# VectorE takes a block of exps ahead of the low parts of K, V, Q and the output products

## What is computed

```
x = layernorm(x + causal self attention(x))      32 heads of 16, rope
q = x Wq + bq                                    32 query heads of 128, 256 rows
k, v = split(context Wkv + bkv)                  8 K and V heads, 4 query heads to each
a = softmax(q k' / sqrt(128))                    over 1601 keys
x = layernorm(x + (a v) Wo + bo)
x = layernorm(x + x Wb' + top-2-of-28 experts' low-rank products)
```

## Time and profile before

| | us |
|---|---|
| median of three runs | 2960.67 |
| lowest, highest | 2955.37, 2963.62 |
| the profiled execution | 2956.6 |
| its span, first to last instruction | 2954.8 |

### The profile page before, as it was taken

How to read it: one execution, slowest core, us unless ns; L and a number is a source line. 1 busy time by engine, 2 the same in 40 slices (tenths; PEclk the granted TensorE clock), 3 DMA queues, 4 the chain that set the end, 5 groups by cost and what they waited for, 6 DMA issues and landing times.

```text
span 2954.8 us, 60508 instructions
## 1 busy us (share of the span) xinstructions
PE 2760.3 (93%) x20272; PEld 2576.1 (87%) x20272; DVE 2100.3 (71%) x4364; ACT 1973.2 (67%) x4392; POOL 1660.6 (56%) x1663
## 2 busy tenths in 40 slices
PE   7899999998899999999899999999988999999996
PEld 6789999998679999999768999999967899999995
DVE  5477777778557878787755877777766587878785
ACT  4476676767457777677655877777756576767673
POOL 4288897947115656565611656555552265656564
PEclk9999999999899999999999999999989999999998
DMA  5446464612311212121331112121232121212112
GB/s 186 139 165 216 160 231 158 211 58 101 119 48 44 94 51 94 51 94 51 122 102 44 63 67 76 69 74 71 78 119 86 42 74 57 89 55 90 55 55 100
DMA packets 97921, 285.10 MB, mean 96 GB/s; under 512 B 9936, under 2 KB 18256, under 8 KB 94416
## 3 DMA queue, kind: packets, MB, share of 16 engines
q1 hardware_dynamic: 97616, 281.24, 27.3%
HBM read 237.16 MB, written 44.04 MB: 95 GB/s over the span
## 4 chain that ended last, share of the span: by engine, by line
PE 67%; issue 11%; POOL 9%; ACT 5%; DVE 5%; DMA 2%; DVEq 0%; ACTq 0%; SPq 0%; POOLq 0%
PE bank L1030 39%; PE dn L1030 14%; PE sp L1030 9%; POOL kept_s L527 4%; ACT ph L714 2%; PE sp L1161 1%; POOL orw L546 1%; PE sp L1169 1%; POOL ol L550 1%; ACT pn L641 1%; PE sp L1101 1%; PE sp L1248 1%; DVE mcol L909 1%; POOL hib L517 1%; ACT sp L719 1%
## 5 line engine op out<-in xcount | busy, mean ns | idle before, releaser
L527 POOL TENSOR_TENSOR kept_s<-kept_s,mrow 128x512 f32<-128x512 f32 (+1 forms) x896 | 1062.3, 1215 | 596.8 <-ACT mrow L704 596.7
L920 DVE TENSOR_TENSOR pl<-sp,ph 128x512 fp32r<-128x512 f32 (+1 forms) x896 | 576.9, 644 | 79.3 <-ACT sp L719 75.8
L714 ACT ACTIVATE ph<-kept_s 128x512 fp32r<-128x512 f32 (+1 forms) x896 | 534.1, 596 | 45.7 <-POOL kept_s L527 42.8
L719 ACT ACTIVATE sp<-kept_s 128x512 f32<-128x512 f32 (+1 forms) x896 | 506.1, 565 | 2.1 <-DVE sua L928 2.1
L1030 PE MATMUL dn<-ph,vh 128*128 128x256 f32 (+1 forms) x1664 | 489.4, 294 | 2.2 <-DVE pl L920 1.7
L1030 PE MATMUL dn<-ph,vl 128*128 128x256 f32 (+1 forms) x1664 | 471.4, 283 | 0.0
L1030 PE MATMUL dn<-pl,vh 128*128 128x256 f32 (+1 forms) x1664 | 470.7, 283 | 0.0
L928 DVE TENSOR_TENSOR sua<-sp,sua 128x512 f32<-128x512 f32 (+1 forms) x640 | 400.2, 625 | 0.0
L696 ACT ACTIVATE kept_s<-bank 128x512 f32<-128x512 f32 x384 | 228.5, 595 | 232.0 <-PE bank L1030 231.4
L696 ACT ACTIVATE kept_s<-sp 128x512 f32<-128x512 f32 x384 | 228.6, 595 | 193.0 <-PE sp L1030 192.6
L1030 PEld LDWEIGHTS dn<-ph,vh 128*128 128x128 f32 (+1 forms) x1664 | 316.5, 190 | 10.3 <-DVE pl L920 3.4
(11 more groups left out here) (149 smaller groups left out, 6967.4 us busy)
## 6 DMA issues: line engine op xcount, KB each, us to landing
wqx<-wq SPq DMA_DIRECT2D x128, 512.0 KB, 3.3
wox<-wo SPq DMA_DIRECT2D x64, 1024.0 KB, 4.8
wk<-wk SPq DMA_DIRECT2D x32, 512.0 KB, 3.3
wvx<-wv SPq DMA_DIRECT2D x16, 1024.0 KB, 5.6
raw<-in_ctx_t SPq DMA_DIRECT2D x48, 200.0 KB, 2.4
wqk<-in_ws SPq DMA_DIRECT2D x17, 513.0 KB, 4.0
raw<-in_wq_in SPq DMA_DIRECT2D x32, 256.0 KB, 3.8
wq<-hib SPq DMA_DIRECT2D x32, 256.0 KB, 2.0
```

Source lines behind the costliest of these rows:

```text
L527: nc.gpsimd.tensor_tensor(kept_s[:, n % 2, i:z, :], kept_s[:, n % 2, i:z, :], mrow[:, n % 2, :].unsqueeze(1).broadcast_to([P, z - i, S]), ...
L714: nc.scalar.activation(ph[:, k % PH, 0:cols], src, ACT.Exp, scale=XSCALE).then_inc(ph_ok, 1)
L719: nc.scalar.activation(pbank[k % 2][:, 0:cols], src, ACT.Exp, scale=XSCALE).then_inc(pr_ok, 1)
L920: nc.vector.tensor_tensor(pl[:, k % PH, 0:cols], src, ph[:, k % PH, 0:cols], ALU.subtract).then_inc(pl_ok, 1)
```

## The change

In each slot of VectorE's list, `low_and_sum` of block g+2 now stands ahead of the `job_low` calls for the jobs of slot g-1. Nothing else is changed, and no wait is added or removed.

```diff
@@ -952,10 +952,10 @@
                 dve.wait_ge(bias_ok, at(b, 2 * TB, 2 * TB))
                 job_low("Q", 0, 0)
                 for g in SLOTS:
+                    for h, s in slot_of(g, LOW):
+                        low_and_sum(h, s)
                     for j in JOBS.get(g - 1, ()):
                         job_low(*j)
-                    for h, s in slot_of(g, LOW):
-                        low_and_sum(h, s)
                     for h in head_of(g, MAX_COL):
                         row_maxima(h)
                     for h in head_of(g, SUM_COL):
```

## The result

| | before | after |
|---|---|---|
| median | 2962.14 (2955.37 to 2965.03, 4 runs) | 2983.87 (2980.64 to 2988.18, 4 runs) |
| ratio, with its 95% interval | | 1.0078 (1.0056 to 1.0100) |
| the profiled execution | 2956.6 | 2980.64 |
| its span | 2954.8 | 2978.6 |
| mean granted clock of TensorE | 0.979 | 0.978 |

The kernel became slower by 21.7 us of the medians; the profiled executions lie 24.0 us apart. The forecast was 2987.7, 27.0 above before; for the profiled execution it was 2983.6, 3.0 more than measured.

What follows compares the result with a forecast made beforehand. TensorE, busy 572 of 590 us in batch 1's cross-attention stage, was taken as the bound. Terms 14.4 + 5.3 + 2.4 + 2.2 = 24.3, with the clock 27.0, on 2960.7 gave 2987.7 us; overall range 2971 to 3001.

Steps and rivals of the forecast that it cites:

- Part 1: V jobs at slots 56, 112, 168: TensorE waits 1.20 us longer for V 6's low part, 12 times, 14.4 us.
- rival (b): No change: TensorE's new waits are taken out of later waits, leaving 8.3 us, 2961 to 2969; 11 in 100.
- Part 2: Slots 28, 84, 140, 196: output product now stands ahead of a reciprocal, 0.41 us later, 13 times, 5.3 us.
- Part 3: End of each batch, slots 215 and 216: output product stands behind a low part, 0.60 us, 4 times, 2.4 us.
- Part 4: Start of each batch: V 11's low part makes TensorE's Q job late, 0.56 us net, 4 times, 2.2 us.
- Gains: Column maxima up to 1.19 us sooner behind K or V jobs, but nothing won: 0, at most 1 us for all.
- Rival (a): Faster: VectorE stops idling for high parts, column maxima come sooner, their waits go, up to 20 us: 2940; 4 in 100.
- The clock: Half clock after some of the twelve new waits of 1.36 us, 1.5 us each: 2.7 us, between 0 and 18.
- Rival (c): Half clock after each of the twelve new waits, 42.7 us in all: 3003; 8 in 100.

Runs made afterwards that it cites:

- part 1 alone: The kernel before, with the new order in slots 56, 112 and 168 of each batch only: 2980.68 us, ratio 1.0082.
- parts 1 and 4 alone: The changed kernel with output products added ahead of the exps' low part again, as before the change: 2979.88 us, ratio 1.0062.
- the two on the fast base: Kernel before with reciprocals and column maxima first where no job is near, plus new order in slots 56, 112, 168 (2910.91 us) or everywhere (2927.79 us).
- before once more: The kernel before, unchanged, run again for a second trace: 2958.3 us in one run.

## Why the prediction was right

**Part 1** (14.4). Twelve waits went from 0.16 to 1.36 us as worked out, and the stretch around each grew by 1.19: 14.3 us. Undone they go, alone they come, half of it costs half, and on a kernel without the other waits they cost the same 1.2. That the next wait of 0.51 us on the reciprocals gives nothing back was the step with which rival (b) would have won. It holds: the stretch up to slot 62 and the ones behind it kept the whole of the loss, and part 1 alone still shows this wait at its old size, batch 2:

```profile
1803.29 0.32 PE L1253 MATMUL sp<-cst,rs 128*128 128x128 f32 x1 [0.51 <-DVE rs L935]
```

The price of a step in VectorE's queue was taken from start to start. The other one, by the DRAIN section of the Trainium skill's VectorE: DVE Perf Modes, would have made it 1.36 for the pair (the same section adds that an instruction that isn't held starts earlier, which the prediction left out): the waits of 0.16, 0.76 and 1.36 us are 0.60 apart, so for these instructions the rows decide against it.

**Part 2** (5.3 predicted). The four places are the right ones, slots 28, 84, 140 and 196, and the waits are 0.35 to 0.37 us where 0.41 was worked out. The reciprocal does come 0.41 us later, but the 0.06 us that TensorE had to spare, read off in the same sentence, had to be taken from it; I left that out. That is the mis-sized term: 0.35, not 0.41. Twelve in batches 1 to 3 make 4.3 us, the one in batch 0 another 0.36 (74.03 against 73.67). In batch 0 waits of 0.35 and 0.37 us came at slots 28 and 140 too, where I had foreseen none; behind slot 140 the wait for GpSimd's fold took it up, and the stretch kept its length (112.85 against 112.86). 4.7 us in all.

**Part 3** (2.4). The last stretch went from 29.02 to 29.62 or 29.63 in all four batches: 0.60 each, to the hundredth.

**Part 4** (2.2). The Q job waits 0.71 us where 0.9 was worked out, and the maxima's wait shrank from 0.61 to 0.36. The first stretch of batch 2, which has no fall in either kernel, grew by 0.85, of which 0.36 are slot 28's: 0.5 for this part against 0.56. With the output products back ahead (batches 1 and 2 at 150.34 and 150.38) it is the same 0.5. Three batches show it; in batch 0 it is lost in larger differences.

**Gains** (0). With the output products back ahead, so that only K, V and Q jobs are moved, the stretches 62 to 106 and 118 to 162 take 109.05 and 109.04 us, where before has 109.15 or 109.13 and 109.08: a tenth or less, some 0.2 us a batch. VectorE's idle time went to other waits. Rival (a) priced a chain through VectorE's queue that isn't there; with the maxima really put ahead of low and sum the same waits did go, so they can be had, but not by this change.

**The clock** (2.7). The place was wrong and the size too small: 6.1 us, batch 0's fall with it, lie within the 0 to 18 but are over twice the 2.7. So this step of the prediction failed although the sum didn't. Batches 1 to 3 have six falls instead of three, 4.6 us. I had put them behind the new waits. Of those twelve one shows a fall (slot 168 of batch 0); at slot 56 of batch 1 the clock is full right behind the wait. The six falls of batches 1 to 3 come behind waits of 1.10 us that the kernel before has too, at slots 77 and 133, in each batch alike. Batch 1, behind the waits at slots 56, 77 and 133:

```profile
1044.80:1048.30 3.50, 3.50 (x30) 3.50 (x31) 2.45 (x6) 0.86 (x2) 2.06 (x3) 1.00 0.02 5
1101.50:1105.00 3.50, 3.50 (x20) 3.50 (x20) 3.50 (x8) 2.07 (x5) 3.50 (x4) 0.58 0.01 1
1251.90:1255.40 3.50, 3.43 (x18) 3.44 (x19) 3.50 (x8) 2.22 (x6) 3.50 (x4) 0.55 0.00 0
```

Over the five profiled executions with waits of 1.36 us (after, parts 1 and 4 alone, part 1 alone, and the two on the fast base) 14 of 60 waits had a fall behind them, 0.23 for each; I had taken 5 in 34, 0.15. But the spread is what counts: 1, 3, 4, 0 and 6 of twelve. Rival (c), with all twelve, came nearest in the execution with six. The Trainium skill's TensorE: Matmul & The Clock Gate, in its section on what is actually happening, ties the lower clock to idling; the falls behind waits of 1.1 to 1.4 us, with TensorE busy before and after, show that such short ones can be enough.

**Batch 0** (about 5 predicted, 1.6 measured). Its first stretch became 5.0 us shorter, 162.07 to 157.09. That isn't the change: part 1 alone, which leaves this stretch in the order of before, has 157.18, while before once more has 161.74. In all of them TensorE waits here for GpSimd's folds, which stand in GpSimd's queue among the splitting of the weights, and these waits differ from run to run. What makes them differ I haven't shown. Without the first stretch batch 0 grew by 6.6 us: 3.6 of part 1, 0.4 and 0.6 of parts 2 and 3, one fall, and some 0.5 in stretches with waits for folds.

**The sum.** 14.3 + 4.7 + 2.4 + 1.5 (part 4 in three batches) = 22.9 for the work, 24.3 predicted; falls 4.6 + 1.5 = 6.1 against 2.7; less the 5.0 us of batch 0's start and 0.4 outside. That makes 23.6 of the 23.8 us by which the spans differ. Had batch 0's start not happened to be short, the profiled execution would have lain at 2986. So the terms for VectorE's order are right by their mechanism, but that the total lies within some us of the forecast is in part luck: 3.4 us too little for the falls stand against 5.0 us in batch 0 that no term foresaw.

## What to carry to other kernels

In a queue that runs in order, work moved ahead costs the start-to-start time of its instructions, and only at the few places where someone's cover behind it is thinner than that: here nine places a batch carried the whole loss that isn't the clock's. So go through the covers slot by slot, and don't argue from the engine's total idle time, which here only changed its place. What belongs ahead of bulk work are the short steps of a long chain: one reciprocal of 0.16 us and one maximum put ahead of low and sum took 2.2% off.

## What the runs showed that I had not expected

Falls of the clock settle into a pattern. In the kernel after they come behind the same two waits in every one of batches 1 to 3, which makes the three stages 595.2 to 595.3 us; in the kernel before, which has the same waits, there were 2, 0 and 1 falls, at slots 21 and 133 and at slot 21, and the stages took 586.1 to 589.3 us. With another order they come behind other waits, even where the waits themselves haven't changed, and their number varies: 3 and 5 in two executions of the same kernel before, 6 after, 11 with part 1 alone, each worth 1.5 us but for those at the very end of a batch, which cost 1.1 or nothing. The length of a wait alone doesn't say whether one comes (none of twelve behind 1.36 us in one kernel, six of twelve in another); what else decides stays open. With the reciprocals put first, the waits of 1.1 us in mid-batch were gone, and so were all falls in batches 1 to 3 and the differences between these batches.
